# Decoder layer, one core: attention's masked terms and quotients spread over the partitions by transfers through DRAM instead of TensorE transposes

## What is computed

```python
kqv = (x @ Wqkv + bqkv).reshape(b, s, 3, 16, 32)
q, k, v = kqv[:, :, 0], kqv[:, :, 1], kqv[:, :, 2]
scores = jnp.einsum('bsnh,btnh->bnst', k, q) / math.sqrt(32)
scores = jnp.triu(scores) + -10000.0 * jnp.tril(ones, k=-1)
attn = jax.nn.softmax(scores, axis=2)
out = jnp.einsum('bnkq,bknh->bqnh', attn, v)
return out.reshape(b, s, 512) @ Wo + bo
```

## Time and profile before

| | |
|---|---|
| time, median of 3 runs | 710.17 us (708.37 to 712.4) |
| the profiled execution: span | 709.9 us, mean granted clock 0.989 |
| attention, groups 0 to 15 | from the start to about 390 us |
| PE / weight loads / DVE / ACT / POOL busy over the span | 671.4 / 380.8 / 513.2 / 496.1 / 395.7 us |
| DMA | 54.33 MB, mean 77 GB/s |

### The profile page before, as it was taken

How to read it: one execution, slowest core, us unless ns; L and a number is a source line. 1 busy time by engine, 2 the same in 40 slices (tenths; PEclk the granted TensorE clock), 3 DMA queues, 4 the chain that set the end, 5 groups by cost and what they waited for, 6 DMA issues and landing times.

```text
span 709.9 us, 12525 instructions
## 1 busy us (share of the span) xinstructions
PE 671.4 (95%) x4290; PEld 380.8 (54%) x4290; DVE 513.2 (72%) x1220; ACT 496.1 (70%) x1143; POOL 395.7 (56%) x508
## 2 busy tenths in 40 slices
PE   8979999899988989799989999999999999999996
PEld 3435555445445545454445454544456797578845
DVE  4676767787888899989755569858777786655644
ACT  5798889789897879978787873384754855336620
POOL 6035735846999664864596654885771634103321
PEclk9999999999999999989999999999999999999999
DMA  7878944322332136460071002000001000000001
GB/s 239 249 218 235 217 145 135 98 75 79 124 102 78 38 85 163 120 143 16 8 120 60 1 0 75 16 31 0 1 1 44 17 1 2 30 31 1 1 16 45
DMA packets 45024, 54.33 MB, mean 77 GB/s; under 512 B 5921, under 2 KB 33825, under 8 KB 44961
## 3 DMA queue, kind: packets, MB, share of 16 engines
q1 hardware_dynamic: 41264, 46.85, 21.6%
q0 software_dynamic: 3264, 6.29, 5.4%
q10 hardware_dynamic: 432, 0.39, 0.2%
HBM read 45.00 MB, written 12.71 MB: 81 GB/s over the span
## 4 chain that ended last, share of the span: by engine, by line
PE 61%; DVE 13%; ACT 10%; POOL 5%; issue 5%; DMA 4%; SPq 1%; POOLq 0%; DVEq 0%; ACTq 0%
PE psb L1160 12%; PE psb L1133 8%; PE psb L996 6%; PE psb L1184 5%; PE psb L1182 5%; PE psb L1104 4%; PE psb L1072 4%; PE psb L1027 4%; DVE ee L1530 3%; PE psb L1039 3%; PE psb L1056 3%; DVE x L1607 2%; PE psb L1120 2%; PE psb L1083 2%; ACT L1330 1%
## 5 line engine op out<-in xcount | busy, mean ns | idle before, releaser
L1530 DVE CUSTOM_DVE_ANT_0 ee<-psb,mask,clip 128x512 f32<-128x512 f32 (+3 forms) x256 | 131.3, 542 | 24.9 <-PE psb L1039 22.3
L1278 ACT ACTIVATE ee<-ee,nm 128x512 f32<-128x512 f32 (+3 forms) x256 | 142.2, 560 | 1.4 <-DVE nm L1530 1.4
L1938 POOL TENSOR_TENSOR hl<-ring,hh 128x512 f16<-128x512 f32 x64 | 80.1, 1264 | 86.7 <-ACT hh L1414 57.3
L1288 ACT ACTIVATE ee<-psb 128x256 f32<-128x256 f32 (+1 forms) x192 | 94.6, 523 | 31.0 <-PE psb L1056 21.0
L1182 PE MATMUL psb<-wd,hh 128*128 128x512 f16 x240 | 91.0, 379 | 0.0
L1184 PE MATMUL psb<-wd,hl 128*128 128x512 f16 x240 | 91.0, 379 | 0.0
L1868 POOL TENSOR_SCALAR_AFFINE_SELECT ee<-ee 128x256 f32<-128x256 f32 x128 | 56.8, 452 | 60.7 <-ACT ee L1288 59.9
L1039 PE MATMUL psb<-ks,qs 128*128 128x512 f16 (+3 forms) x256 | 72.5, 305 | 8.3 <-DVE nm L1530 6.1
L1056 PE MATMUL psb<-qs,ks 128*128 128x128 f16 (+3 forms) x256 | 60.1, 306 | 9.6 <-ACT ee L1288 7.5
L996 PE MATMUL psb<-xh,wqk 128*128 128x512 f16 x240 | 61.8, 385 | 1.7 <-POOL xh L1830 1.2
L1885 POOL TENSOR_TENSOR rs<-ve,half 128x1 f32<-128x1 f32 (+1 forms) x24 | 20.5, 854 | 72.0 <-DVE ve L1599 71.7
(11 more groups left out here) (217 smaller groups left out, 1668.2 us busy)
## 6 DMA issues: line engine op xcount, KB each, us to landing
qs<-parts SPq DMA_DIRECT2D x48, 128.0 KB, 2.7
ks<-parts SPq DMA_DIRECT2D x45, 128.0 KB, 2.9
parts<-qhl SPq DMA_DIRECT2D x16, 256.0 KB, 2.2
parts<-khl SPq DMA_DIRECT2D x16, 256.0 KB, 2.2
x<-in_x SPq DMA_DIRECT2D x4, 1024.0 KB, 6.8
ct<-in_ctxT SPq DMA_DIRECT2D x4, 1024.0 KB, 5.1
out<-x SPq DMA_DIRECT2D x16, 256.0 KB, 2.0
xt<-in_xT SPq DMA_DIRECT2D x14, 256.0 KB, 3.4
```

The costliest lines, as they stand in the source:

```text
L1278: e.activation(dst, dst, ACT.Exp, bias=NM[:, n % 4, col:col + 1], scale=-1.0, accum_out=DEN[:, n % 4, col:col + 1]).then_inc(sem("exp"), 1)
L1288: e.activation(ET[H % ET_SLOTS][:, base:base + width], PSB[:, bank["turn", H, item], 0:width], ACT.Exp, scale=SC).then_inc(sem("et"), 1)
L1530: e.tensor_tensor_reduce(E[H % E_SLOTS][:, EOFF[i]:EOFF[i] + w], PSB[:, bank["score", H, i], 0:w], MASK[:, S - w:S], -SC, CLIP[:, i:i + 1] ...
L1938: e.tensor_tensor(HS[it][1][:], pair(b, it // 2)[:, it % 2, :] if b in SEVEN else ring(b, it)[1], HS[it][0][:], ALU.subtract).then_inc(sem ...
```

## The change

EM and the denominators now lie side by side in one tile ED (128 x 2 x 16), of which PE turns 128x32 at once to 32 rows x 128 (`rows`, one transpose). ACT copies the 32 rows (`rowcopy`), SP writes them to DRAM (`rput`, 16 KB), waits for that, and reads the masked terms back, each head's row over 32 partitions, into WIDE (`emb`, four transfers of 64 KB). After `t1`, SP reads the quotients over the same WIDE (`rb`, four transfers); after `t3` the next group's masked terms may follow. `t1` reads WIDE and writes EB, `t3` reads WIDE. The multiplication by SOME is gone; the last column of EB, the only token without a masked one, is set to zero by POOL after `ol`. `expand`, `widen` and `eb` are gone. NM has 2 slots for 4. The numbers of the timetable are set anew.

```diff
-EX_AT = {0: 21, 1: 45, 2: 58, 3: 77, 4: 89, 5: 99, 6: 123, 7: 140, 8: 155, 9: 170, 10: 189, 11: 208, 12: 214, 13:
...
+EX_AT = {0: 20, 1: 44, 2: 58, 3: 76, 4: 85, 5: 99, 6: 121, 7: 132, 8: 151, 9: 169, 10: 181, 11: 204, 12: 213, 13: 236,
...
-REST_AT = (5, 28, 96, 16)
+REST_AT = (5, 29, 96, 17)
...
-    "spread": lambda n, which: ("t3", n) if which else ("eb", n),
+    "rows": lambda n: ("rowcopy", n),
...
-    def spread(n, which):
-        tt.unit("spread", n, which)
-        add("spread", n, which)
-        if which == 0:
-            add("widen", n)
-            late(WAIT["eb"], lambda: add("eb", n))
+    def row_values(n):
+        add("expand", n)
+        late(WAIT["rows"], lambda: rows(n))
+
+    def rows(n):
+        tt.unit("rows", n)
+        add("rows", n)
+        add("rowcopy", n)
+        add("rput", n)
+        masked_rows(n)
+
+    def masked_rows(n):
+        if ("rput", n) in tt.place and (n == 0 or ("t3", n - 1) in tt.place):
+            add("emb", n)
...
-        late(WAIT["t1"], lambda: add("t1", n))
+        late(WAIT["t1"], lambda: (add("t1", n), add("rb", n)))
...
+        def rows(n):
+            emptied(("rows", n))
+            pe.wait_ge(*by("emx", n))
+            pe.wait_ge(*by("expand", n))
+            pe.wait_ge(*by_consts())
+            e.transpose(PSB[0:32, bank["rows", n], 0:P], ED[:, n % 2, :, :].rearrange("p k c -> p (k c)"),
+                        IDENT[:]).then_inc(sem("rows"), 1)
...
+        def row_copy(n):
+            act.wait_ge(*by("rows", n))
+            if n:
+                act.wait_ge(sem("rput"), 16 * n)
+            e.activation(ROWS[:], PSB[0:32, bank["rows", n], 0:P], ACT.Copy).then_inc(sem("rowcopy"), 1)
...
+            dve.wait_ge(*by_masked_rows(n))
+            if n:
+                dve.wait_ge(*by("ol", n - 1))
+            e.tensor_tensor(EB[:, 3 * P - 1:S - 1], sums[:, 3 * P:S], WIDE[:, 3 * P - 1:S - 1], ALU.mult)
...
+            dve.wait_ge(*by_quotients(n))
+            e.tensor_tensor(EB[:], EB[:], WIDE[:], ALU.mult).then_inc(sem("t3"), 1)
...
+        def put_rows(n):
+            sp.wait_ge(*by("rowcopy", n))
+            e.dma_start(RSCR[n].rearrange("k h (i t) -> (k h i) t", i=T), ROWS[:]).then_inc(sem("rput"), 16)
+
+        def spread_rows(n, k, name):
+            for h in range(4):
+                e.dma_start(WIDE[32 * h:32 * h + 32, :],
+                            RSCR[n, k, h].unsqueeze(0).broadcast_to([32, S])).then_inc(sem(name), 16)
+
+        def masked_rows(n):
+            sp.wait_ge(sem("rput"), 16 * (n + 1))
+            if n:
+                sp.wait_ge(*by("t3", n - 1))
+            spread_rows(n, 0, "emb")
+
+        def quotients(n):
+            sp.wait_ge(*by("t1", n))
+            spread_rows(n, 1, "rb")
```

More of the change, by code:

```diff
@@ L606, in close @@
     def close(n):
-        spread(n, 1)
-        late(WAIT["t3"], lambda: add("t3", n))
+        late(WAIT["t3"], lambda: (add("t3", n), masked_rows(n + 1) if n < NG - 1 else None))
         late(WAIT["oh"], lambda: add("oh", n))
@@ L613, in timetable @@
     for n in range(NG):
-        for slot, what in ((EX_AT[n], lambda n=n: add("expand", n)), (SV_AT[n], lambda n=n: value_sums(n)),
-                           (SPREAD_AT[n], lambda n=n: spread(n, 0)), (PV_AT[n], lambda n=n: values(n)),
+        for slot, what in ((EX_AT[n], lambda n=n: row_values(n)), (SV_AT[n], lambda n=n: value_sums(n)),
+                           (PV_AT[n], lambda n=n: values(n)),
                            (WIDE_AT[n], lambda n=n: close(n))):
@@ L1085, in sv @@
             mm.then_inc(sem("sv"), 1)
-        def spread(n, which):
-            emptied(("spread", n, which))
-            pe.wait_ge(sem("rx" if which else "ex"), n + 1)
-            src = WIDE
-            for i in range(T):
-                mm = e.transpose(PSB[:, bank["spread", n, which], i * P:(i + 1) * P], src[:, i * P:(i + 1) * P], IDENT[:])
-            mm.then_inc(sem(f"spread{which}"), 1)
+        def rows(n):
[5 more added lines that the diff above has]
+                        IDENT[:]).then_inc(sem("rows"), 1)
         def wo_part(b, t, p):
@@ L1209, in _ @@
                 sv(*a)
-            elif name == "spread":
-                spread(*a)
+            elif name == "rows":
+                rows(*a)
             elif name == "wo":
@@ L2062, in _ @@
                 put_shifts(*a)
+            elif name == "rput":
+                put_rows(*a)
+            elif name == "emb":
+                masked_rows(*a)
+            elif name == "rb":
+                quotients(*a)
             elif name == "load_rest":
```

159 lines of the change are left out of this document (71 added, 88 removed), and 17 rows, old and new, of the table TURN_AT.

## The result

The change makes the kernel slower: 719.86 us median (718.50 to 720.30) against 711.28 (708.37 to 713.31) for the kernel before on the same chip, ratio 1.0136 with a 95% interval of 1.0098 to 1.0173. The span of the profiled execution is 718.4 us. The span of before, 709.9, therefore belongs to a run of some 711.6 us and not, as the prediction took it, to one 0.2 us above the span. That is near the median on this chip: the two spans differ by 8.5 us, the two medians by 8.6. The experiments ran on other chips, where before has medians of 708.9 to 710.1 us; beside their ratios its profile stands 1.5 to 2.7 us too slow.

A forecast was written before the change was run, and what follows sets the result against it. It saw no engine alone bounding attention and used the chain of waits, more than half PE's. Terms -7.1 - 0.5 - 1.5 + 1.1 + 1.2 + 0.5 + 0 + 0 = -6.3 us gave span 703.6, median 703.8; range 696 to 712.

The forecast's parts named there:

- Terms 1 to 4: In attention: 128 transposes gone -7.1 us, ACT's EB copy gone -0.5, POOL's widening gone -1.5, sixteen row transposes added +1.1.
- the rival with DVE and ACT as the bound: In attention, PE's time isn't asked for: -0.3 us, 709.8 us, between 707 and 712; chance 0.19.
- The chain's share of L1092: Eight transposes a group hold 2.1% of the chain from 50 to 390 us, 7.1 us, taken as the gain from removal.
- Term 5: Way through DRAM: 4.8 us from issue of rows to WIDE filled, refill 3.4; +1.2 and +0.5 us at few places, otherwise nothing.
- (a): Group 14: rows stand behind group 15's shifts, WIDE filled 2.5 us late for `t1`; between 0 and +2.5, taken +1.2 us.
- (b): Group 11: 3.6 us between `t1` and `t3` for a refill of 3.4; between 0 and +1, taken +0.5 us.
- Term 6: SP's queue: nine more transfers per group, 3.5 us of issue, plus waits; -1.2 against +1.2, set at 0, between -2.4 and +3.
- place 1: Spot in SP's queue with thin cover: about 4.9 us of issue and wait added where SP had idled under 2 us.
- SP's queue is in order: Maxima's transfers late behind the new ones, PE stops at a group's first `turn`: +7.2 us, 717 us; chance 0.14.
- Term 7: Timetable anew, most pieces moved one to four slots, DVE's own work unchanged: 0, with 2 us either way.

The follow-up runs named there:

- e_before_traffic: The kernel before with the 27 transfers of groups 0 to 2 added on SP's queue, read by no one: 715.62 us, one run.
- e_before_t3sbuf: The kernel before with `t3` multiplying by a constant SBUF tile in place of the quotients in PSUM, division left out: 711.31 us, ratio 1.0025.
- e_rput_act_wu: The change with the rows' small write issued by ACT and the four 512 KB loads of `wu` moved to groups 4 and 5: 718.88 us, ratio 1.0126.
- e_before_pe2x: The kernel before with each of the 32 units of four transposes done twice, 14.1 us of PE more: 719.90 us, ratio 1.0142.
- e_rput_act: The change with the rows' small write issued by ACT instead of SP, which still waits for its landing: 713.46 us, ratio 1.0078.
- e_pe_all: The change's timetable with before's mechanism, all 16 groups by PE transposes and no row through DRAM: 733.70 us, ratio 1.0334.

## Why the prediction was wrong

The forecast was 703.8 us with 700 to 707 for its case, and a range of 696 to 712; measured were 719.9. Part of the gains came, and a loss of 10.6 to 15.5 us stood where the text had 0.

**Terms 1 to 4.** The new work is near what was stated: row transposes of 273 ns with their latency, the copy of the rows 251 ns. PE has 9.2 us less to do, where 14.1 - 2.2 = 11.9 was reckoned. From group 4 on the change gains 3.2 + 2.8 = 6.0 us beside the forecast's -8.0 for these terms. Only the last part is clear of the scatter: from group 15 to the end before, `e_before_traffic` and `e_before_t3sbuf` take 383.5 to 383.8 us, the change and eight of the versions with the last groups through DRAM 380.3 to 381.6. (`e_rput_act_wu` and the three with only groups 0 to 2 on PE take 383.0 to 385.4, which stays open.) Between 4 and 15 the same three kernels take 230.3 to 232.4 us, so that the 3.2 isn't clear of it. And the reason was not a half of PE's time all along: `e_before_pe2x` shows 0.9 to 3.0 of 9.7 us in the middle, where the rival with DVE and ACT as the bound was nearer, and about PE's full time at the ends. The chain's share of L1092 doesn't measure what removing it is worth, since the next wait stands just behind it.

**Term 5, the step that failed.** "The timetable leaves more than that nearly everywhere ... Nothing is added to `t1` of the others." The way was costed by medians, 1.4 us for the write and 2.2 for a fill. In group 1 the rows left 4.4 us after they were ready, the write took 6.1, and the four fills 3.7 where 3.4 was reckoned: 14.2 us in place of 4.8. With the 4.4 gone, in `e_rput_act`, it was still 13.3, now with slow fills: the mis-sized term is the landings, beside large loads and behind what the queue had just issued. DVE's waits for WIDE came to 10.3 + 4.0 = 14.3 us, where the text named more than 3 as the sign of this failure. The text had the DMA share of 0.78 in that stretch and said that transfers "may be slower there", then gave it no number. Places (a) and (b) that it did price are minor: DVE's waits for WIDE from 160 us to the end of attention sum to 1.6 us. The write landed in 1.4 us at best, 2.5 in the median and 6.1 at worst.

The Trainium skill (DMA: Bandwidth & Descriptors, section "Anatomy of one DMA") would not have shown it either: its fixed cost of about 2 us is fitted there to transfers that GpSimd issues, these are SP's, and the trace has them on both sides of it.

**Term 6.** Set at 0 between -2.4 and +3. The thin cover at place 1 was seen, but priced wrongly: the 4.9 us count all nine transfers of a group, of which only the write and four fills stand there, 0.33 + 1.4 + 4 x 0.4 = 3.3 us by the same rows and 54.46 - 50.35 = 4.1 in the trace. The maxima leave 4.1 us later (1.9 of it lost before), and their landing is 2.2 us longer. The `xt` load that was to give 1.2 us back is what they then land behind. The rival named "SP's queue is in order" had the right queue, and its sign for the failure, `qs<-shifts` growing from 1.4 us to 5 or more, came true with 6.6; but `e_pe_all` shows 6.8 without any rows, so that sign proves little. That its price, 717 us, came near is luck: it had 1.5 us in each of 9 groups at `turn`, where the loss lies in three early groups, at the maxima of group 1 and at `t1` of group 1. The chance of 0.14 was too low; that a wait for a landing blocks everything behind it in that queue, and that the landing itself waits for what was issued ahead of it, called for the worst landing of that stretch, not the median.

**Term 7.** The timetable can't be priced by itself: the new slots with the old mechanism are 3.3% slower than before, the old slots with the new mechanism 7.4% (one run). "DVE's own work is unchanged, as `t1` and `t3` keep their shapes" was wrong: the shape is the same, the operand's memory isn't, and it costs 15.1 - 10.7 = 4.4 us of DVE, 0.25% in `e_before_t3sbuf`.

**Still open:** how the rest of the early loss in `e_rput_act` (5.9 us from 1 to 4) divides between slow landings, the new slots and scatter of the first groups; and why single loads in groups 8 to 11 cost as much as they do. A second buffer for WIDE, which would let the fills start a group earlier, was not tried.

## To carry to other kernels

Cost a transfer that someone waits for by the landings in its own stretch, and by what its queue issues just ahead of it, not by the kernel's median: here 1.4 us became 3.4 to 6.1. The DMA share alone doesn't tell: the 3.4 came at a share of 0.44 (50 to 60 us), 0.5 us behind a load of 256 KB. When a write, its landing and a read back go into an in-order queue that already carries such a round trip, count the wait for the other one's landing, in both directions, or issue the write from the engine that produces the data. A share of the chain tells what an operation held up, not what its removal gives; doubling it, read by stretches and with more than one profile of each kernel, tells in which parts its engine's time is asked for.
